# Column parts of the second product in another order, the x sums of the second block product held back, and one LoRA-B copy moved from VectorE to ScalarE

## The reference

```python
x = x + (x @ weight.T + bias + scale[a] * (x @ lora_a[a].T) @ lora_b[a].T)   # a: id 1, 8 adapters
x = x + x @ w[c].T                                                          # c: id 2, 16 adapters
# x (32, 128, 2048), weight (2048, 2048), w (16, 2048, 2048), all float32
```

## Time and profile before

| | |
|---|---|
| median of three runs | 2750.38 us (2745.59 to 2751.7) |
| profiled execution | 2752.24 us, span 2750.4 us |
| PE busy | 2718.7 us, 99% of the span, 12057 matmuls |
| DVE busy | 1822.5 us, 66% |
| ACT busy | 1339.7 us, 49% |
| POOL busy | 738.8 us, 27% |
| granted PE clock, mean | 0.998 |

### The profile page before, as it was taken

The page is one execution under the profiler, slowest core; times in us unless marked ns, Lnnn a source line. Parts: engine busy times, 40 slices in busy tenths (PEclk is TensorE's granted clock), DMA queues, the critical chain, the costliest instruction groups (busy, mean ns, idle before and its releaser), DMA issues.

```text
span 2750.4 us, 34206 instructions
## 1 busy us (share of the span) xinstructions
PE 2718.7 (99%) x12057; PEld 2246.1 (82%) x12057; DVE 1822.5 (66%) x1628; ACT 1339.7 (49%) x1413; POOL 738.8 (27%) x589
## 2 busy tenths in 40 slices
PE   8999999999999999999999999999999999999999
PEld 6788888888888888888888888888888888888887
DVE  6767776866665657686756565768675646666766
ACT  3333355756442336666643232666664323356665
POOL 4345711411612111141251221114134112111321
PEclk9999999999999999999999999999999999999999
DMA  8858956666845435666784543899997554499997
GB/s 297 327 198 294 334 167 216 218 210 225 315 159 194 154 113 190 208 221 212 231 304 156 191 157 131 295 302 315 314 323 271 173 174 163 142 305 313 303 321 246
DMA packets 198108, 645.17 MB, mean 235 GB/s; under 512 B 23185, under 2 KB 33585, under 8 KB 197937
## 3 DMA queue, kind: packets, MB, share of 16 engines
q1 hardware_dynamic: 197936, 642.98, 68.9%
HBM read 651.28 MB, written 58.72 MB: 258 GB/s over the span
## 4 chain that ended last, share of the span: by engine, by line
PE 89%; DVE 4%; DMA 3%; POOL 2%; ACT 1%; issue 1%; SPq 1%; ACTq 0%; POOLq 0%; DVEq 0%
PE acc L855 16%; PE acc L857 16%; PE acc L856 16%; PE acc L801 13%; PE acc L812 13%; PE acc L802 13%; DMA raw<-w 3%; DVE ws L736 2%; PE acc L772 2%; POOL raw L519 1%; POOL raw L502 1%; PE acc L810 1%; DVE ops L736 1%; DMA raw<-xt 1%; ACT ws L607 0%
## 5 line engine op out<-in xcount | busy, mean ns | idle before, releaser
L736 DVE TENSOR_TENSOR ws<-raw,ws 128x1024 fp32r<-128x1024 f32 (+1 forms) x1008 | 1304.6, 1317 | 430.6 <-ACT ws L607 426.9
L607 ACT CAST ws<-raw 128x1024 fp32r<-128x1024 f32 (+1 forms) x1008 | 1027.7, 1044 | 1145.0 <-PE acc L812 516.5
L855 PE MATMUL acc<-ws,ops 128*128 128x512 f32 (+1 forms) x2048 | 798.2, 390 | 6.8 <-DVE ws L736 6.6
L856 PE MATMUL acc<-ws,ops 128*128 128x512 f32 (+1 forms) x2048 | 796.9, 389 | 0.0
L857 PE MATMUL acc<-ws,ops 128*128 128x512 f32 (+1 forms) x2048 | 796.8, 389 | 0.0
L801 PE MATMUL acc<-ops,ws 128*128 128x512 f32 x1792 | 700.8, 391 | 13.2 <-DVE ops L736 6.8
L812 PE MATMUL acc<-ops,ws 128*128 128x512 f32 x1792 | 699.8, 391 | 0.0
L802 PE MATMUL acc<-ops,ws 128*128 128x512 f32 x1792 | 698.8, 390 | 0.0
L519 POOL TENSOR_TENSOR raw<-raw,eye_s 128x128 f32<-128x128 f32 x384 | 358.6, 965 | 1257.3 <-DMA raw<-w 1256.7
L502 POOL TENSOR_TENSOR raw<-raw 128x1024 f32<-128x1024 f32 (+1 forms) x116 | 309.0, 2664 | 561.6 <-DMA raw<-xt 463.8
L855 PEld LDWEIGHTS acc<-ws,ops 128*128 128x128 f32 x2048 | 384.4, 188 | 90.7 <-issue 7.7
(11 more groups left out here) (60 smaller groups left out, 660.3 us busy)
## 6 DMA issues: line engine op xcount, KB each, us to landing
raw<-w SPq DMA_DIRECT2D x928, 512.0 KB
raw<-xt SPq DMA_DIRECT2D x172, 512.0 KB
raw<-w_sums SPq DMA_DIRECT2D x104, 512.0 KB
out<-ost SPq DMA_DIRECT2D x128, 256.0 KB, 5.8
w_sums<-raw SPq DMA_DIRECT2D x32, 512.0 KB, 5.0
x_sums<-raw SPq DMA_DIRECT2D x16, 512.0 KB, 3.9
raw<-x_sums SPq DMA_DIRECT2D x16, 512.0 KB
raw<-a SPq DMA_DIRECT2D x80, 64.0 KB
```

The source lines that it names most:

```text
L607: ins = eng.copy(hi, src)
L736: ins = eng.tensor_tensor(lo, src, hi, ALU.subtract) if hi is not None else eng.tensor_copy(lo, src)
L855: eng.matmul(acc, yh, wh, start=begin, stop=False)
L856: eng.matmul(acc, yh, wl, start=False, stop=False)
```

## The change

Three parts.

1. A table `PART = (1, 0, 3, 2)`: step kc of the second product computes column part PART[kc]. Weight address, output address and the units that take the identity follow. Those are now units 2, 3 in step 0, units 0, 1 in step 1, units 6, 7 in step 2 and units 4, 5 in step 3.
2. In the groups g = 1 to 3, POOL waits for the last matmul of group g-1's second product before its first x sum for the second block product (`X g,1,0`).
3. The LoRA-B split writes the hi part three times instead of twice on ACT, and DVE no longer makes the third copy. That is 32 copies of 32x1024 in all.

```diff
+PART = (1, 0, 3, 2)
 ...
         g, h, kc, u, j = index
-        return ["eye2"] if u // 2 == kc else []
+        return ["eye2"] if u // 2 == PART[kc] else []
 ...
-                eng.dma_start(out[bass.ds(batch, 1), :, kc * 512:(kc + 1) * 512].rearrange("a p n -> (a p) n"),
+                eng.dma_start(out[bass.ds(batch, 1), :, PART[kc] * 512:PART[kc] * 512 + 512].rearrange("a p n -> (a p) n"),
 ...
-                    src = w1[bass.ds(order(q, 1)[j + (j > 0)], 1), kc, u].rearrange("a p n -> (a p) n")
+                    src = w1[bass.ds(order(q, 1)[j + (j > 0)], 1), PART[kc], u].rearrange("a p n -> (a p) n")
 ...
             for n, (_, _, kind, index) in enumerate(splits):
                 steps = pool_steps(kind, index)
+                if kind == "X" and index[0] and index[1] == 1 and index[2] == 0:
+                    eng.wait_ge(s_mm, at["S", index[0] - 1, 1, C1 - 1, NU - 1, 2] + 1)
 ...
-                return [(src, dst[0:32]), (src, dst[32:64])], [(src, None, dst[96:128]), (src, dst[0:32], dst[64:96])]
+                return [(src, dst[r:r + 32]) for r in (32, 96, 0)], [(src, dst[0:32], dst[64:96])]
 ...
-                    ins = eng.tensor_tensor(lo, src, hi, ALU.subtract) if hi is not None else eng.tensor_copy(lo, src)
+                    ins = eng.tensor_tensor(lo, src, hi, ALU.subtract)
```

## The result

| us | median | lowest to highest | ratio to before (95%) |
|---|---|---|---|
| before, 8 runs | 2751.04 | 2745.59 to 2757.05 | |
| after, 8 runs | 2741.76 | 2739.20 to 2745.33 | 0.9969 (0.9959 to 0.9978) |

A forecast was written before the change was run, and what follows sets the result against it. PE, busy 99%, was taken as the bound, so only its lost time counts. Terms -7.1 - 4.0 - 0.4 + 0.8 + 0.2 = -10.5 took 2752.24 to 2741.7, lowered to 2741.0 us; 8-in-10 range 2736 to 2749.

The forecast's parts named there:

- First part of h = 1, -7.1: Second product, four groups: with identity gone from its front, the late weight tile's cast comes earlier, saving 7.1 of 7.46 us.
- rival 1: First part of h = 1 keeps its loss because ACT's Y cast and evictions make the tile late; 2749 us, chance 0.07.
- Last part, -4.0: Last part of h = 1, groups 0 to 2: identity at units 4, 5, not 6, 7, saves 4.0 of 4.42 us.
- The idle 2.69 us of the earlier trace: Group 2's last part: POOL stood idle 2.69 us for a weight tile with late DMA, and everything behind it followed.
- Hold, -0.4: Starts of groups 1 to 3: POOL's wait before the first x sum shortens its chain, leaving 0.6 of 0.97 us lost.
- The 11.29 us of that chain: Before, from first x sum to PE's third weight tile, against 10.88 us PE gives; the hold was to make it about 10.4.
- Rival 2: The hold binds: chain steps at the group starts take their slow length, +12.3 us and not +0.6; 2753 us, chance 0.07.
- First part of h = 0, +0.8: Identity at units 2, 3 falls where DVE is full, costing 0.2 us in each of four groups.
- 6 x 0.27: First part of h = 0: about six of twelve identity operations each slow DVE by 0.27 us, 1.6 us together.
- LoRA, +0.2: 32 LoRA-B copies move from DVE to ACT; only in group 0 can this reach PE, between -0.5 and +1.0 us.
- Rival 3: Slower: in eight first parts each identity operation holds DVE its full 0.44 us, +29 instead of +0.8; 2769 us, chance 0.05.

The follow-up runs named there:

- e2: The hold alone put on the kernel before, with the old part order and old LoRA-B copy; 2750.19 us, ratio 1.0000.
- e3: The LoRA-B copy move to ACT alone, put on the kernel before; 2752.36 us, ratio 1.0007.
- e5: The changed kernel with PART = (1, 0, 2, 3), so identity is again at units 6, 7 in step 3; 2744.91 us, ratio 0.9980.
- e1: The new order of column parts alone: the changed kernel without the hold and with DVE's LoRA-B copy back; 2741.79 us, ratio 0.9971.
- e9: e4 with the stores of x and weight sums one raw place earlier (SAVE_AFTER 4 in place of 5); 2748.54 us, ratio 0.9994.
- e10: e1 with the stores of x and weight sums one raw place earlier (SAVE_AFTER 4 in place of 5); 2748.34 us, ratio 0.9987.
- e7: The changed kernel with POOL's identity operation twice as wide, doubling 256 columns instead of adding the identity; 2749.54 us in one run.
- e4: The changed kernel with only the LoRA-B move taken back, so new part order plus hold; 2738.86 us, ratio 0.9957.
- e12: e4 with the stores of x and weight sums earlier still (SAVE_AFTER 3 in place of 5); 2772.97 us, ratio 1.0079.

## Why the prediction was right, point by point

*First part of h = 1, -7.1: the mechanism is shown.* It measured -7.0 in the profile; the cast came at T+0.87, and ACT's wait for POOL and PE's for DVE were gone. The size rests on one execution of before: of the two others with the old order one lost 7.3 us there and one 5.5. Parts alone gave the whole change of the median, and rival 1 (ACT and its evictions make the tile late) falls, since the evictions are still there and PE does not wait. The guess that the rest would lie in group 2 was right in kind: 0.23 us stay in the part ahead of h = 1 in groups 2 and 3. One sign failed without a cost: ACT was never to wait for POOL in these parts, and did once, 0.72 us in group 2.

*Last part, -4.0: right in place and direction, its size taken from one execution, one of its two reasons wrong.* The profile went from 4.4 to 0. But 1.8 us of that were group 2's x sum, which in that execution started just ahead of a subtraction; e2 and e3 lose 2.4 us in these parts of three groups together, so that the change in the medians is likely nearer to -2.5. The idle 2.69 us of the earlier trace rows, on which the prediction had everything follow, stand in e2 with a loss of 1.3. The prediction did name the x sum's early start, and wrote its cost to this row; e5, which puts the identity back at that one place, measured +3.2 for this part and the next group's start together.

*Hold, -0.4: wrong as a cause, and the term too small.* The starts lost 1.0 and now lose 0. The step that failed is that the wait would shorten POOL's chain: without it the chain is as short (e1, sum ready at T+4.64), because the identity work in front is gone, and with it but with that work back the starts lose 1.5 us (e5). The hold's worth is not above what 22 runs resolve (e9 against e10), nor 11 alone (e2). The 11.29 us of that chain count from the sum's own start; from T it was 11.38. Rival 2, that it binds, fails too: POOL's first pair took 4.92 us and not 6.9.

*First part of h = 0, +0.8: measured 0.* The term that was too large is 6 x 0.27. About six of the twelve operations do fall behind T, as reckoned, but they do not all meet a subtraction. POOL in that place in group 1, T = 1034.94:

```profile
1019.31 2.76 POOL L522 TENSOR_TENSOR raw<-raw,eye_s 128x128 f32<-128x128 f32 x2 [55.47 <-DMA raw<-w]
1025.37 2.27 POOL L522 TENSOR_TENSOR raw<-raw,eye_s 128x128 f32<-128x128 f32 x4 [3.29 <-DMA raw<-w]
1035.35 0.88 POOL L522 TENSOR_TENSOR raw<-raw,eye_s 128x128 f32<-128x128 f32 x2 [7.71 <-DMA raw<-w]
1037.34 3.69 POOL L522 TENSOR_TENSOR raw<-raw,eye_s 128x128 f32<-128x128 f32 x4 [1.12 <-DMA raw<-w]
```

All were done by T+6.1, six of them before T. DVE beside them:

```profile
1037.38 1.51 DVE L739 TENSOR_TENSOR ops<-cb,ops 128x1024 fp32r<-128x1024 f32 x1
...
1040.63 1.48 DVE L739 TENSOR_TENSOR ops<-cb,ops 128x1024 fp32r<-128x1024 f32 x1
1042.04 2.35 DVE L739 TENSOR_TENSOR ws<-raw,ws 128x1024 fp32r<-128x1024 f32 x2
```

And the same weight tiles in before:

```profile
1044.02 2.36 DVE L736 TENSOR_TENSOR ws<-raw,ws 128x1024 fp32r<-128x1024 f32 x2 [0.49 <-ACT ws L607]
```

Of the six behind T four took 0.46 us, beside DVE's additions out of PSUM or at the very end of a subtraction, and two took 1.44. Only the two subtractions beside these were longer, by 0.29 and 0.26; I had reckoned with six. Those 0.55 us went into the pause of 0.49 that DVE had at T+7.07 before and has no more, so that from T+7.1 on it stands as before: the row with unit 2's third tile begins at T+12.77 (before T+12.75).

*LoRA, +0.2: not resolved.* Its bounds of -0.5 and +1.0 hold the 0.6 between pooled medians, but a cost of up to 2 us is not ruled out. That DVE waits for ACT's third copy is shown (e3); that PE pays for it is not.

*Rival 3.* The price of an identity operation to DVE stays 0.27 (0.26 and 0.29 above), and in after no first part of h = 0 or h = 1 pays for it. e7 shows that this is near the limit: at 0.42, and with POOL's rows as much longer, PE loses 11.4 us behind group 0's first product, where after loses 3.9.

*The sum.* -10.5 from the profiled execution of before was forecast; -11.4 was measured between the two profiles and -9.3 between medians. That 2741.0 came within 0.8 us of 2741.76 is in part luck. In the profile the last part (-4.4) and the group starts (-1.0) gave 1.0 us more than forecast and the first part of h = 0 cost 0.8 less, while group 0's first product lost 0.9 us more than forecast. There before, e1, e2 and e4, whose programs are the same there, differ by up to 4.4 us, so that this last term is within the noise.

## What to carry to other kernels

Where two engines exclude each other, look for where their common work stands in unbroken runs, and not at how much there is of it: here the same 384 operations cost 5.5 to 7.5 us where twelve tiles that need them followed each other, another 3 where six stood right ahead of the next group's tiles and x sums, and almost nothing where they stood apart. An edit that acts at the place of a loss need not be what removes it: only leaving the hold out showed that it did nothing there. And a loss read from one execution can be a matter of tenths of a microsecond between two engines; here 1.8 of 3.2 us were, as two further traces of the same piece of work show.

## What the runs showed of the hardware

Behind some pauses PE runs seven or eight matmuls at half pace. In after at 107.47, and the stretch from 108 us with its granted clock (the 0.50 behind the busy times):

```profile
107.47 0.50 PE L804 MATMUL acc<-ops,ws 128*128 128x512 f32 x1 [2.96 <-DVE ws L739]
...
108.59 0.63 PE L804 MATMUL acc<-ops,ws 128*128 128x512 f32 x1
109.02 0.63 PE L805 MATMUL acc<-ops,ws 128*128 128x512 f32 x1
```

```profile
108.00:111.00 3.00, 3.00 (x8) 2.32 (x8) 1.89 (x3) 1.81 (x2) 0.00 (x0) 0.50 0.54 187
```

And e4 at the same place:

```profile
106.63 0.50 PE L804 MATMUL acc<-ops,ws 128*128 128x512 f32 x1 [2.05 <-DVE ws L739]
...
107.21 0.39 PE L815 MATMUL acc<-ops,ws 128*128 128x512 f32 x1
107.44 0.40 PE L804 MATMUL acc<-ops,ws 128*128 128x512 f32 x1
```

The step is 0.43 us in the first (the 1.2 GHz level) and 0.23 in the second (2.4 GHz). That costs some 1.5 us each time, and e4's mean granted clock was 1.000 where after's was 0.998. Behind 100 us, before, e1 and after had one such stretch each, at different places, and e4 none, while e9 had two, with 18 slow matmuls, and e12 with its longer pauses went down to a clock of 0.89 in one block. A stretch more or less is a part of what makes runs of one kernel differ (15 us over 28 runs of before): the eleven of them with a mean clock of 0.997 took 2751.8 us on average, the six with 0.999 took 2749.2. Whether it explains e4's lower median was not tried.
